# Second score product of a head over 64 rows, two heads side by side

## The reference

```python
logits = einsum('bqhmd,bkhd->bhmqk', q, k) * SM_SCALE     # first attention, q and k rotated
logits = where(causal and within 128 keys, logits, -inf)
m = max(logits);  e = exp(logits - m)
w = e / (sum(e) + exp(sink - m));  out = einsum('bhmqk,bkhd->bqhmd', w, v) @ out_w.T + out_b

scores = einsum('bhqd,bhkd->bhqk', q, repeat(k, 4)) / sqrt(64)   # second attention, causal only
out = softmax(where(causal, scores, min)) @ repeat(v, 4) @ wo
```

## Time and profile before

| | |
|---|---|
| Median of 3 runs | 1061.11 us (1060.68 to 1061.96) |
| Profiled execution, span from the first to the last instruction | 1063.1 us |
| Mean granted clock of TensorE | 0.962 of full speed |
| TensorE busy (weight loads) | 965.1 us, 91% (901.5 us) |
| VectorE, ScalarE, GpSimd busy | 789.4, 753.5 and 466.7 us |
| Score products (L1053) | 1024, mean 317 ns |
| Mask and maximum (L1734) | 512, mean 435 ns |

### The profile page before, as it was taken

How to read it: one execution, slowest core, us unless ns; L and a number is a source line. 1 busy time by engine, 2 the same in 40 slices (tenths; PEclk the granted TensorE clock), 3 DMA queues, 4 the chain that set the end, 5 groups by cost and what they waited for, 6 DMA issues and landing times.

```text
span 1063.1 us, 22951 instructions
## 1 busy us (share of the span) xinstructions
PE 965.1 (91%) x6862; PEld 901.5 (85%) x6862; DVE 789.4 (74%) x2308; ACT 753.5 (71%) x2122; POOL 466.7 (44%) x550
## 2 busy tenths in 40 slices
PE   5589999999899899999999999999998589999991
PEld 3379899998789799988999999999887489999991
DVE  6779998989899577777777777777764756666646
ACT  3368788887888688788888778877884346555641
POOL 4346668777656333433444332232222852222243
PEclk8899999999999899999999999999997699999996
DMA  8799879787476675465557455354303365555313
GB/s 178 185 233 274 208 190 276 209 213 201 112 177 147 167 190 155 122 164 135 136 140 166 122 168 120 110 153 126 71 1 120 115 221 172 166 170 162 103 58 116
DMA packets 146059, 166.18 MB, mean 156 GB/s; under 512 B 79194, under 2 KB 100714, under 8 KB 140816
## 3 DMA queue, kind: packets, MB, share of 16 engines
q1 hardware_dynamic: 129440, 143.58, 52.0%
q0 software_dynamic: 3712, 11.16, 3.3%
q10 hardware_dynamic: 12784, 9.97, 3.0%
HBM read 105.88 MB, written 58.79 MB: 155 GB/s over the span
## 4 chain that ended last, share of the span: by engine, by line
PE 56%; DVE 17%; issue 10%; ACT 9%; DMA 4%; POOL 1%; SPq 1%; DVEq 0%; ACTq 0%; POOLq 0%
PE psO L1086 14%; PE psS L1053 10%; PE psX L1063 8%; PE psY L1102 6%; PE psP L985 6%; ACT wgt_hi L1319 3%; DVE pbuf L1734 2%; DVE gated L2074 2%; DVE pTl L1756 2%; PE psO L1069 2%; PE psS L1236 2%; PE psP L998 2%; ACT relu_s L1624 2%; PE psX L1236 1%; DVE den L1748 1%
## 5 line engine op out<-in xcount | busy, mean ns | idle before, releaser
L1351 ACT ACTIVATE pbuf<-pbuf,nmax 128x256 f32<-128x256 f32 (+3 forms) x512 | 264.9, 519 | 45.8 <-DVE nmax L1734 44.7
L1053 PE MATMUL psS<-kT,qE 128*128 128x256 f32 (+3 forms) x1024 | 238.2, 317 | 25.7 <-DVE nmax L1734 24.1
L1734 DVE CUSTOM_DVE_ANT_0 pbuf<-psS,mcau 128x256 f32<-128x256 f32 (+3 forms) x512 | 219.9, 435 | 46.9 <-PE psS L1053 41.0
L1756 DVE TENSOR_TENSOR pTl<-psX,pTh 128x512 fp32r<-128x512 f32 x272 | 187.1, 688 | 73.5 <-ACT pTh L1319 72.9
L1319 ACT ACTIVATE pTh<-psX 128x512 fp32r<-128x512 f32 x272 | 160.7, 591 | 55.7 <-PE psO L1086 39.3
L1053 PEld LDWEIGHTS psS<-kT,qE 128*128 128x128 f32 x1024 | 160.2, 192 | 40.3 <-DVE nmax L1734 33.7
L1086 PE MATMUL psO<-pTh,vpad 128*128 128x256 f32 x1088 | 187.1, 294 | 3.2 <-DVE oS L1762 2.0
L798 POOL TENSOR_TENSOR ol<-oS,oh 128x256 fp32r<-128x256 f32 x128 | 94.8, 741 | 200.7 <-ACT oh L1319 196.2
L1063 PE MATMUL psX<-idn,pbuf 128*128 128x128 f32 x1088 | 162.2, 274 | 3.1 <-DVE pTl L1756 3.1
L1086 PEld LDWEIGHTS psO<-pTh,vpad 128*128 128x128 f32 x1088 | 150.3, 190 | 10.5 <-DVE oS L1762 5.4
L1063 PEld LDWEIGHTS psX<-idn,pbuf 128*128 128x128 f32 x1088 | 126.5, 141 | 9.4 <-DVE pTl L1756 3.3
(11 more groups left out here) (295 smaller groups left out, 2369.0 us busy)
## 6 DMA issues: line engine op xcount, KB each, us to landing
qd<-st SPq DMA_DIRECT2D x32, 1024.0 KB, 4.5
qE<-qd SPq DMA_DIRECT2D x128, 256.0 KB, 6.0
mrawV<-in_w_moe SPq DMA_DIRECT2D x32, 384.0 KB
mrawB<-in_w_moe SPq DMA_DIRECT2D x32, 384.0 KB
kT<-kd SPq DMA_DIRECT2D x64, 128.0 KB, 4.4
kT<-kd SPq DMA_DIRECT2D x32, 256.0 KB, 4.3
kd<-st SPq DMA_DIRECT2D x7, 1024.0 KB, 4.8
xg<-sq ACTq DMA_DIRECT2D x7, 640.0 KB, 6.1
```

Of the source, the lines that this page charges most:

```text
L1053: last = mm(psS[j % 2][:, 0:n], qE[:, g % 2, j, t * P:(t + 1) * P], kT[:, g % 2, c, k0:k0 + n], start=(c == 0), stop=(c == 1))
L1351: nc.scalar.activation(pj, pj, ACT.Exp, bias=nmax[:, u % 4, j:j + 1], scale=-1.0, accum_out=sums[:, u % 4, j:j + 1]).then_inc(a_exp, 1)
L1734: V.tensor_tensor_reduce(probs(u, j), psS[j % 2][:, 0:n], mcau[:, SEQ - n:], -SCALE, 3e38, ALU.add, ALU.min, nmax[:, u % 4, j:j + 1]).then ...
L1756: V.tensor_tensor(pTl[:, kt % 2, :], psX[kt % 2][:, :], pTh[:, kt % 2, :], ALU.subtract).then_inc(v_pl, 1)
```

## The change

A head's first score product stays over 128 rows. Its second one, with the low part of the keys, now runs over the 64 rows that hold the high part of the queries, so the product of low queries with low keys is left out. So that two heads can use the two row halves of the array, odd heads have high and low part exchanged in `qE`: `place_q` places even and odd heads in DMAs of their own. In the first attention that makes 8 DMAs a group in place of 4, each of half the size; in the second attention it stays at 4, and the count of the semaphore `ld_q` is set to 128 a group in both.

`scores` now takes a pair of heads: the two whole products into the two banks, then the two half products. It waits until `v_max` has reached the first head of the pair, that is until both banks have been read. Each half product signals its own head. In `step_window` and `step_causal` the first pair stands where head 0 stood; the second pair stands behind `turn_scale` in `step_window`, and where head 3 stood in `step_causal`. The orders of the other engines are as before.

```diff
             def place_q(g):
...
-                wait(sp, ld_q, 64 * g)
+                wait(sp, ld_q, 128 * g)
...
                     for i in range(4):
-                        sp.dma_start(qE[32 * i:32 * i + 32, slot, :, :].bitcast(F32),
-                                     qd[slot, :, i, :].rearrange("(j d) n -> d j n", j=QM)).then_inc(ld_q, 16)
+                        heads = qd[slot, :, i, :].rearrange("(j d) n -> d j n", j=QM)
+                        for r in range(2):
+                            at = 32 * (i if r == 0 else (i + 2) % 4)
+                            sp.dma_start(qE[at:at + 32, slot, r:r + 3:2, :].bitcast(F32), heads[:, r:r + 3:2, :]).then_inc(ld_q, 16)
                 else:
                     for c in range(2):
                         for r in range(2):
-                            dst = qE[64 * c:64 * c + 64, slot, :, :].rearrange("p (i r) n -> p i r n", r=2)[:, :, r, :]
-                            sp.dma_start(dst.bitcast(F32), qd[slot, 64 * r:64 * r + 64, 2 * c:2 * c + 2, :]).then_inc(ld_q, 16)
+                            at = 64 * (c if r == 0 else 1 - c)
+                            dst = qE[at:at + 64, slot, :, :].rearrange("p (i r) n -> p i r n", r=2)[:, :, r, :]
+                            sp.dma_start(dst.bitcast(F32), qd[slot, 64 * r:64 * r + 64, 2 * c:2 * c + 2, :]).then_inc(ld_q, 32)
...
-            def scores(u, j):
-                h = QM * u + j
-                wait(pe, v_max, h - 1)
+            def scores(u, pair):
+                h = QM * u + 2 * pair
+                wait(pe, v_max, h)
...
-                for c in range(2):
-                    last = mm(psS[j % 2][:, 0:n], qE[:, g % 2, j, t * P:(t + 1) * P], kT[:, g % 2, c, k0:k0 + n],
-                              start=(c == 0), stop=(c == 1))
-                last.then_inc(s_S, 1)
+                for r in range(2):
+                    mm(psS[r][:, 0:n], qE[:, g % 2, 2 * pair + r, t * P:(t + 1) * P], kT[:, g % 2, 0, k0:k0 + n],
+                       start=True, stop=False)
+                for r in range(2):
+                    half = slice(2 * HALF * r, 2 * HALF * r + 2 * HALF)
+                    mm(psS[r][:, 0:n], qE[half, g % 2, 2 * pair + r, t * P:(t + 1) * P], kT[half, g % 2, 1, k0:k0 + n],
+                       start=False, stop=True).then_inc(s_S, 1)
...
             def step_window(u):
...
-                scores(u, 1)
                 if u >= 3:
                     turn_scale(u - 3)
-                scores(u, 2)
+                scores(u, 1)
                 if u >= 5:
                     out_project(u - 5)
-                scores(u, 3)
                 if ahead(u):
                     project(ahead(u))
...
             def step_causal(u):
...
                 if nk > 0:
                     turn_probs(u - 2, 0)
-                if now:
-                    scores(u, 1)
...
-                if now:
-                    scores(u, 2)
                 if u - 3 < NU:
                     turn_scale(u - 3)
                 if nk > 1:
                     turn_probs(u - 2, 1)
                 if now:
-                    scores(u, 3)
+                    scores(u, 1)
```

More of the change, by code:

```diff
@@ L518, in store_q @@
                     sp.wait_ge(v_pj, ITEM["q", g, 1])
-                wait(sp, ld_q, 64 * (g - 1))
+                wait(sp, ld_q, 128 * (g - 1))
                 sp.dma_start(qd[g % 2], st[:, :, :, :].bitcast(F32).rearrange("p c r n -> p (c r) n")).then_inc(st_out, 16)
@@ L1040, in project @@
                     turn_features(index)
-            def scores(u, j):
-                h = QM * u + j
-                wait(pe, v_max, h - 1)
+            def scores(u, pair):
+                h = QM * u + 2 * pair
+                wait(pe, v_max, h)
                 g = u // TB
-                if j == 0 and u % TB == 0:
-                    pe.wait_ge(ld_q, 64 * (g + 1))
+                if pair == 0 and u % TB == 0:
+                    pe.wait_ge(ld_q, 128 * (g + 1))
                     pe.wait_ge(ld_kt, 64 * min(g + 1, NG // 2) + 32 * max(g + 1 - NG // 2, 0))
```

## The result

The changed kernel takes 1190.16 us in the median (1187.63 to 1195.63), the kernel before 1061.32 beside it: a ratio of 1.1225 with the 95% interval [1.1191, 1.126]. The forecast was 1098 with a range up to 1148; the direction was right, and the size was too small by a factor of 3.5 (+129 against +37).

The account below looks back on a forecast made before the run. TensorE was taken to bound the causal half, the order of TensorE and VectorE within a step the windowed one. Windowed +33, causal +3 and first steps +1 gave +37: 1098 us beside the runs, range 1064 to 1148.

Parts of the forecast that it names:

- Step (a): Windowed half: first pair waits for the last maximum, closing a loop; +26 to +33, taken +33, bounds 0 and +52 us.
- Step (b): Score pairs: half products share a slot, saving at most 0.11 to 0.233 us a pair, at most 20 us causal.
- Step (c): Causal half: three-key steps without projection lose, one- and two-key steps -7 to 0; bounds -10 and +13, taken +3 us.
- Step (d): Windowed step: VectorE's 0.76 us wait for head 1 goes but returns ahead of head 2; nothing saved beyond the loop.
- Step (e): Query placement on SyncE's queue: 64 more DMA issues, 1.7 us on each of 16 placements, covered: 0; uncovered +22.
- The clock: Sign of being right: the granted clock stays at 1.00, since the new gaps are about 1 us.
- Rival 2: Switching between whole and half rows empties the array: 0.16 us a switch, +60 in all, 1158 us; chance 0.18.
- Rival 3: The halves don't run side by side: windowed +37, causal +13, start +1, 1112 us; chance 0.15.
- Rivals 1 and 4: TensorE alone sets the pace, 1026 or 1044, chance 0.12; new waits swallow VectorE's surplus, within 0.2% of 1061, chance 0.05.

Follow-up runs that it names:

- e1: Changed kernel with second score products over all 128 rows again, its order, wait and eight placing DMAs kept: 1142.2 us, ratio 1.0778 to the kernel before.
- e10: e1 with VectorE adding the denominators behind head 1's maximum instead of ahead of it: 1136.0 us, ratio 1.0694 to the kernel before.
- e9: Kernel before, whole rows and old order, with only the pair's wait for both banks added: 1167.6 us, ratio 1.1022.
- e2: e1 with four placing DMAs a group, as in the kernel before, instead of eight: 1144.5 us, ratio 1.0775 to the kernel before.
- e6: Changed kernel with each pair's two half products issued twice: 1218.2 us, ratio 1.1487 to the kernel before.

## Why the prediction was wrong

**The difference taken apart.** e1 splits the +124.7 of the spans: the wait and the order cost 61.1 in the windowed half and 14.1 in the causal one (e1 less before); the excursions 26.6 and 21.7 (after less e1); the first steps with what lies ahead of them 8.2; the rest gives back 7.0. The sum forecast 33, 3, nothing, nothing, 1 and nothing. Up to 5 of the 26.6 can be clock, since the windowed half was at half clock for 10.2 us more than in e1 (below), of which TensorE can lose half.

**Step (a), the loop: right in its mechanism, mis-sized.** The first pair starts 0.05 us behind the last maximum, VectorE's part sums to 158.3 as forecast (158), the lead to 4.7 (3). The failed term is the head part: 194 to 201 by the forecast (its 197 to 204 less the hand-back), 253.6 measured. It has two errors of about one size.
- *A clean pattern for one half of the loop, a total for the other.* The forecast built the head part from the slots of one undisturbed step, and took VectorE's part as a sum over 60 steps. The head part of the kernel before, measured the same way, was 222.7, of which the shortest step of each kind makes only 193.3; the 29 us above it are a surplus of the other steps. The forecast named the steps in which VectorE is late with a projection as not in its sum, and set nothing for them but the choice of the upper end, 33 of 26 to 33. The surplus stayed: e1, with whole rows, has a clean pattern of 205.1, 4 to 11 over the forecast, and 24.5 above it; the changed kernel 230.2 and 23.3. In e1, 16 of the 24.5 stand in the 28 steps in which VectorE's small sum took over 0.25 us, and e10, which moves the sum, leaves 12.3 of them in the head part.
- *The excursion at nothing.* The step said that going from one kind of product to another "costs nothing visible". That row shows only products over whole rows. By the shortest steps the excursions add 25 us to the head part (230.2 less 205.1).

The bounds 0 to +52 didn't hold: the lead of 52 us was called the upper bound, but the wait with its order costs 61 in the windowed half (e1), and alone in the old order 77 (e9). Here the wait that closes the loop cost more than the lead it took away. The likely reason is that what VectorE does late in one step now delays the next; e10 shows it for a part of the surplus, not for all. The upper end of the range, 1148, is 1061 with 52, 13 and 22 added: it had no room for the switching besides.

**Step (b), the saved slot: real, and never seen.** The halves' starts are 3 ns apart, and the slot goes. The excursion of 0.24 to 0.29 takes back more, at 512 columns, where the slot is longest, still 61 ns more.

**Step (c), the causal half: wrong in size.** +35.8 against +3, outside -10 to +13. Whole rows (e1) give +14.1: the three-key steps +9.2, the four-key ones +6.9, those with one or two keys -2. Three-key steps were named with +5 to +7; the four-key ones were set to nothing on balance. The other 21.7 are excursions, 0.17 for each of 126 pairs beyond the saved slot: the pairs themselves are longer by 15.2, and the products directly behind them hold up their followers by 8.1, of which some is absorbed.

The next step's start in the earlier trace rows against the changed kernel's steps 98 and 99: 3.48 became 4.78, and the first pair of step 99 waits 0.73, as (c) described it ("about 4.5").

```profile
729.02 0.52 PE L1057 MATMUL psS<-kT,qE 128*128 128x384 f32 x2
729.47 0.44 PE L1061 MATMUL psS<-kT,qE 64*128 64x384 f32 x2
...
733.80 0.73 PE L1057 MATMUL psS<-kT,qE 128*128 128x512 f32 x2 [0.73 <-DVE nmax L1735]
```

**Step (d): right.** VectorE's wait for head 1 is gone, and 1.92 us stand ahead of head 2 in step 29, 0.76 stood ahead of head 1.

**Step (e), the DMAs at nothing: right** (e2, 1144.5 with four against 1142.2 with eight).

**The clock: partly wrong.** It was to stay at 1.00. The first four steps ran at a granted clock of 0.63 (0.92 before), half of full speed, 1.2 GHz, for 20.5 of 27.6 us; in the whole stage 19.2 us of TensorE's work were recorded, and the longer of the two falls, at 63.2, came behind a wait of 1.38 us ahead of the first pair at 61.3. The windowed half was at half clock for 23.9 us, before for 10.2. In e1 it was 13.7 us in the first four steps and 13.7 in the windowed half. At most half of the 13.7 us that the changed kernel has more than the kernel before in the windowed half can be lost TensorE time, some 7 (an estimate from the two levels). That the rest is 7.0 shorter goes with 42.6 us at half clock there against 53.3; no run tests either.

**The rivals.** Rival 2 was there, with a price near the one it gave: 0.16 for each switch, 0.32 for an excursion, against 0.24 to 0.29, or 0.3 to 0.4 with the product behind the pair; 60 us in all, against 48.3. The Trainium skill, "TensorEngine Tiling (Array Packing)", section Tiling Modes (Key Properties), says that changing the mode, not just the tile, drains TensorE. The trace agrees as far as it goes: the way in and the way out take 0.09 us each beyond a slot (e6); that the array runs empty in them is not shown. Rival 2 was set beside the forecast as another case with 0.18, when it is another term of the same sum: nothing in (a) excluded it. Rival 3 is refuted (3 ns). Rivals 1 and 4 fall with the lead: TensorE is busy for 85% of the windowed half, no longer 95, and VectorE's surplus stayed on the path. Even rival 2's 1158 is 32 short of the result; the loop's size makes that.

**What stays open.** What the 0.09 us on the way to half rows and the 0.09 on the way back are: an array running empty, or something else that a change of rows costs. Only the other 0.05 to 0.10 of an excursion goes with weight loads that start with their products, since that shows without a change of rows too. And of e1's surplus in the head part, 12.3 of 24.5 us, no run shows the cause; the 12.2 that e10 takes out shorten the windowed half by 6.5 only.

## What to carry to other kernels

Before a wait is widened from one buffer to two, look at the lead it takes away (next start less last release), and size the new loop by sums over all steps on every engine of it; a step picked for being clean leaves out just what the loop no longer absorbs. A product over fewer rows between whole ones has to save more than the way there and back, here 0.24 to 0.29 us against 0.11 to 0.23 saved. By e6, where a further half pair cost one slot and would have replaced two, half products could pay in longer runs of their own; no run here has one that pays. And a mechanism that no row excludes is a term of the sum and not an alternative to it.

## What was not expected of the hardware

- A product whose weight load starts with it, or less than 0.03 us ahead, holds up the next one by 0.03 to 0.10 us more than a slot. All half products of the changed kernel are such (their loads start 1 to 2 ns ahead), whole products behind a wait are too, and the half products of e6's second pairs, whose loads start ahead, are not.
- For the same reason the second whole product of a first pair starts 0.22 behind the first at 256 columns where a slot is 0.12, in e1 as in the changed kernel; a pair of four slots, 0.48 by the forecast, takes 0.58.
- A sum over 128x4 on VectorE takes 0.15 to 0.16 us in most steps, and up to 1.25 in others (24 of 64 over 0.5 us in the kernel before). The long ones end with GpSimd: all that took over 0.25 us, 27 in the kernel before, 28 in the changed one and 30 in e1, began while a GpSimd instruction ran, mostly one of the rotation of queries (L785, L793 before), and ended 16 to 24 ns behind it; of the 107 shorter ones, six began beside one. By these rows a long sum waits for GpSimd. In e1, 16 of the 24.5 us of surplus in the head part stand in steps with such a sum.
